# Counts added by VectorE and transposed by a DMA, and the first layer's output added to x in DRAM by a DMA of GpSimd

## The chip, the cores and the metric

The kernel runs on one core of one Trainium2 chip. The metric is the device time of one execution in microseconds (us), lower is better. The engines are TensorE (PE in the rows, its weight loads PEld), VectorE (DVE), ScalarE (ACT), GpSimd (POOL) and SyncE (SP, which here only issues DMAs).

## What is computed

x has 1250 rows (nodes) of 1024 values, and 20,000 edges go from `src` to `dst`, each of one of two relations. Two graph layers follow one another:

```
h = relu(layernorm(x))                       # layer 1, RGCN with 286 hidden columns
g = t5_norm(h)
z = g @ W_root + bias + sum over r of (sum of g[src] @ W_rel[r] over the edges of r into a node) / max(count, 1)
x1 = x + h + elu(z) @ wo_weight              # x + h is called xh below
h2 = relu(layernorm(x1)) @ W                 # layer 2, graph attention
w(s, d) = exp(-leaky_relu(al[s] + ar[d]))    # once for each edge from s to d
out = x1 + elu(sum of w(s, d) * h2[d] / sum of w(s, d))
```

## The kernel before

**Tiles and counts.** The 1250 rows are ten tiles of 125 (`T`, `TILES`). The kernel does not gather edges. For every tile t of destinations TensorE builds a matrix of counts, how often source s points to destination d in relation r, from one-hot rows that VectorE makes (`rows_of`, two comparisons a group, five groups a tile, `one_hots(g)`). The products of a group (`counted(g)` on TensorE, line 1301) land in one of two PSUM banks. ScalarE copies them out as `adj_hi` (line 579, what the sums of messages use) and casts that copy to 16 bits as `adj_16` (line 583). The group after next needs the bank, so it waits for the first of these copies.

**Layer 1.** A pipeline over the ten tiles, written out by hand with a lag for each stage. In one step TensorE does, in this order: group 0 of tile t; `y_transposed` of tile t-2; `summed(0)` of t-1 (messages of relation 0, line 1340); group 1; `summed(1)`; the first part of the transposed counts of t-1; group 2; the first half of `output1` of t-2 (elu(z) @ wo_weight, lines 1385 to 1388); the second part; group 3; the second half of `output1`; the third part; group 4. Sums of a tile need all five copies of its groups. VectorE computes z (`z_of`) when the sums are there, ScalarE takes its exponential (`elu`), VectorE finishes y (`y_of`), TensorE transposes it and both engines copy it out in two precisions (`y_split`).

**Transposed counts.** The attention layer needs the counts of both relations together, and with sources along the free dimension. In the kernel before TensorE transposes them by multiplying with an identity (`counts_transposed`, line 1363, 20 matrix products a tile in parts of 8, 8 and 4, in PSUM banks 4 and 5, both relations adding up in the bank) and ScalarE copies the three parts to `counts` (`counts_out`, line 599).

**x1.** `xh` lies in DRAM (`xh_scratch`). SyncE loads a tile of it into `xt`, VectorE adds the output of layer 1 from PSUM (`output1`, line 1008), SyncE stores the sum in `x1_scratch`. Layer 2 loads it as `x1t`, and again at the end as `xr`.

**Between the layers.** After the pipeline come written-out calls for the last tiles (`before` is tile 8, `last` is tile 9), mixed with the first two tiles of layer 2: norms (`norm2`, line 629), transposes (`transposed2`, line 1397) and the splitting of the eight blocks of W in two precisions, a cast by ScalarE (line 617) and a difference by VectorE (line 1014). The blocks are loaded by SyncE in the order of `ORDER`: two after `rows_free`, four after the last sums, and the last two and `a_b` after the last transposed counts, since they lie where `adj_16` lay. `products2` (lines 1414 to 1416) then takes the blocks one by one. The transposes of layer 2's tile 2 stand behind `products2` of tile 0 on TensorE.

Of the kernel before, what the change touches and what calls it, by code (L numbers as in the profile page):

```python
# [5 lines left out]
def rgcn_gat_kernel(nc, x, src, dst, edge_type, ln_weight, w_rel, w_root, conv_bias, wo_weight, w_gat, a_gat, out):  # L6
# [5 lines left out]
    N, D = x.shape  # L12
# [93 lines left out]
    spans_dram = nc.dram_tensor("spans_scratch", [SPANS, SPAN], F32, kind="Internal").ap()  # L106
    xh_dram = nc.dram_tensor("xh_scratch", [N, D], F32, kind="Internal").ap()
    x1_dram = nc.dram_tensor("x1_scratch", [N, D], F32, kind="Internal").ap()
# [3 lines left out]
    with ctx:  # L112
# [7 lines left out]
        ident_r = sb(ctx, "ident_r", [P, P], R32)  # L120
# [24 lines left out]
        sb(first_rows_of, "below_ring_first", [P, 3 * N], BF16)  # L145
        ring_first = sb(first_rows_of, "ring_first", [P, FIRST, GW, HOT], BF16)
        first_rows_of.close()
        counts = sb(ctx, "counts", [T, TILES, N], U16)
# [16 lines left out]
        def over(name, within, new, shape):  # L165
# [28 lines left out]
        (adj_lo,), lo_end = lay(at, ("adj_lo", [T, BLOCKS, PAIR], R32))  # L194
        (ring_more, adj_16, ident_16), end2 = lay(at, ("ring_more", [P, MORE, GW, HOT], BF16), ("adj_16", [T, BLOCKS, PAIR], F16),
                                                  ("ident_16", [P, P], F16))
# [41 lines left out]
        def columns(adj, b, g):  # L238
# [9 lines left out]
            last_in list_rdy list_out spans_out xlist_in picks_rdy rows_rdy span_rdy win_in wkeyp_rdy found_rdy total_rdy win_16 hot_ready x_ready dot_rdy  # L248
# [3 lines left out]
        for n in ("x_in", "x_ahead", "xh_out", "xh_ahead", "xb_in", "x1_in", "xr_in", "x1_out", "out_done"):  # L252
            S[n] = [sem(f"{n}{b}") for b in range(2)]
# [23 lines left out]
        def _(sp):  # L277
# [58 lines left out]
            def load_xh(t, b):  # L336
                if t < 2:
                    sp.wait_ge(S["xh_out"][b], came_x(TILES - 2 + b, b))
                else:
                    if t < AHEAD:  # L340
                        sp.wait_ge(S["xh_ahead"][b], 32)
                    sp.wait_ge(S["x1_out"][b], came(t - 2, b))
                move(xt[b], row(xh_dram, t), ("xb_in", b))

            def store_x1(t, b):
                sp.wait_ge(S["x1_rdy"], data(t))
                move(row(x1_dram, t), xt[b], ("x1_out", b))

            def load_x1(t, b):
                sp.wait_ge(S["gT_ps"], room(t))  # L350
                sp.wait_ge(S["x1_out"][b], came(t, b))
                move(x1t[b], row(x1_dram, t), ("x1_in", b))
# [3 lines left out]
            load_xh(0, 0)  # L356
            load_xh(1, 1)
# [6 lines left out]
            for t in range(TILES):  # L364
                if t == 4:
                    load_x1(0, 0)
                    load_x1(1, 1)
                if t == TILES - 2:
                    sp.wait_ge(S["rows_free"], 1)
                    for k in ORDER[0:2]:  # L370
                        load_wg(k)
                    load_x1(2, 0)
                    sp.wait_ge(S["s_ps"], data(TILES - 1))
                    for k in ORDER[2:6]:
                        load_wg(k)
                    sp.wait_ge(S["c_ps"], 3 * data(TILES - 1))
                    for k in ORDER[6:8]:
                        load_wg(k)
                    for first, end in ((0, BAND), (BAND, T)):
                        sp.dma_start(a_b[first:end], a_gat.rearrange("o (s d) -> (o s) d", s=2).partition_broadcast(end - first)).then_inc(S["a_in"], 16)  # L380
                if t == TILES - 1:
                    load_x1(3, 1)
                store_x1(t, t % 2)
                if t + 2 < TILES:
                    load_xh(t + 2, t % 2)
# [8 lines left out]
            def load_xr(t, b):  # L394
                sp.wait_ge(S["out_done"][b], out_room(t, b))
                move(xr[b], row(x1_dram, t), ("xr_in", b))
# [18 lines left out]
        def _(pool):  # L415
# [42 lines left out]
            pipeline((residual, 0), steps=(TILES - 2, TILES))  # L458

# [15 lines left out]
        def _(act):  # L475
# [60 lines left out]
            def pads():  # L536
                A.copy(ident_r[:], ident[:])
# [31 lines left out]
            def counts_evicted(t, b, g, usual=False):  # L569
# [5 lines left out]
                if g == 0:  # L575
                    act.wait_ge(S["s_ps"], room(t))
                    act.wait_ge(S["c_ps"], 3 * room(t))
# [17 lines left out]
            def counts_out(t, b, d, parts=range(3)):  # L595
                for c in parts:
                    act.wait_ge(S["c_ps"], 3 * t + c + 1 + 3 * CREDIT)
                    n = min(4, TILES - 4 * c)
                    A.copy(counts[:, bass.ds(t, 1), 4 * T * c:4 * T * c + n * T].rearrange("p o (n s) -> p (o n) s", s=T),
                           ps[0:T, 4 + c % 2, 0:n * CB].rearrange("p (n s) -> p n s", s=CB)[:, :, 0:T]).then_inc(S["c_used"], 1)  # L600

# [10 lines left out]
            act.sem_inc(S["c_used"], 2 * CREDIT)  # L612

# [25 lines left out]
            def counts_part(c):  # L639
                return lambda t, b, d: counts_out(t, b, d, (c,))  # L640

# [3 lines left out]
            def projected(t, b, d):  # L645
                act.wait_ge(S["diag_rdy"], data(t))
                A.copy(h_hi[:, bass.ds(t, 1), :].rearrange("p o (h n) -> p (o h) n", h=2),
# [8 lines left out]
            def early_weights():  # L656
                act.wait_ge(S["first_v"], 1)
# [35 lines left out]

            with act.If_eq(flag, 0):
                act.wait_ge(S["g_ps"], data(TILES - 1))
                A.copy(ident_16[:], ident[:])
# [19 lines left out]
            with act.If_ne(flag, 0):  # L716
                split_wo()
                with act.Fori(0, TILES // 2) as d:
# [3 lines left out]
                    for b in range(2):  # L722
                        for stage in (counts_out, elu, y_split):
                            stage(d * 2 + b, b, d)
# [787 lines left out]
```

## Time and profile before

| | |
|---|---|
| time, median of 3 runs | 532.98 us (532.26 to 533.81) |
| the profiled execution, its own time | 530.4 us |
| span of its instructions | 528.6 us |
| mean granted clock of TensorE | 0.994 |
| TensorE busy | 502.6 us, 95% |
| VectorE busy | 368.9 us, 70% |
| ScalarE busy | 231.3 us, 44% |
| GpSimd busy | 74.6 us, 14% |

The span runs from the first to the last instruction; the time of the execution has 1.8 us more around it. The preparation and the first products fill the span up to about 119 us, the pipeline of layer 1 runs from there to 240 us, its end is mixed with the start of layer 2 up to about 271 us, and from there on TensorE works through layer 2. A row of the timeline gives start, duration, engine, line and operation, and in brackets how long the engine was idle before it and who ended that.

### The profile page before, as it was taken

The numbers are of one execution on the slowest core, as the hardware profiler recorded it, in microseconds if no ns is written. First come the engines' busy times: TensorE is split into PE (matmuls) and PEld (weight loads), VectorE is DVE, ScalarE is ACT, GpSimd is POOL, SyncE is SP. The second block draws the span as 40 slices with busy tenths as digits, with TensorE's granted clock in tenths as the row PEclk, the third lists the DMA queues.
The fourth block names the chain that finished last, engine by engine and source line by source line (L and its number), as shares of the span: only waits on it lengthen the run. The fifth ranks groups of instructions, "written<-read, shape, count | busy, mean of one in ns | idle before, by whom it ended". The sixth has DMA issues, their size and how long they took to land.

```text
span 528.6 us, 7977 instructions
## 1 busy us (share of the span) xinstructions
PE 502.6 (95%) x3073; PEld 433.2 (82%) x3073; DVE 368.9 (70%) x634; ACT 231.3 (44%) x386; POOL 74.6 (14%) x72
## 2 busy tenths in 40 slices
PE   3989999997899999998999999999999999999995
PEld 2889989997789999998778888888787888888885
DVE  4836885578798888855875555554798887777633
ACT  5855443407856666668733332221333322222112
POOL 1362213100000000000000000000073322222400
PEclk9999999999899999999999999999999999999998
DMA  9862273304013233225951111100022222222211
GB/s 259 223 224 79 78 236 104 118 1 110 1 50 107 81 120 115 79 79 167 311 191 39 40 39 40 39 1 0 1 78 79 78 78 79 78 79 78 79 41 41
DMA packets 22186, 49.15 MB, mean 93 GB/s; under 512 B 4798, under 2 KB 10709, under 8 KB 22018
## 3 DMA queue, kind: packets, MB, share of 16 engines
q1 hardware_dynamic: 21887, 48.33, 30.5%
q8 instruction: 26, 0.43, 0.3%
q0 software_dynamic: 256, 0.26, 0.2%
q14 instruction: 17, 0.14, 0.1%
HBM read 33.05 MB, written 16.85 MB: 94 GB/s over the span
## 4 chain that ended last, share of the span: by engine, by line
PE 84%; DVE 8%; ACT 5%; issue 1%; DMA 1%; SPq 0%; DVEq 0%; ACTq 0%
PE ps L1208 13%; PE ps L1433 9%; PE ps L1340 9%; PE ps L1434 9%; PE ps L1435 9%; PE ps L1414 6%; PE ps L1416 6%; PE ps L1415 6%; PE ps L1301 3%; PE ps L1363 2%; PE ps L1385 2%; PE ps L1397 1%; PE ps L1387 1%; PE ps L1386 1%; PE ps L1234 1%
## 5 line engine op out<-in xcount | busy, mean ns | idle before, releaser
L1433 PE MATMUL ps<-h_hi,att_hi 125*125 125x512 f32 (+1 forms) x190 | 73.5, 387 | 0.0
L1434 PE MATMUL ps<-h_lo,att_hi 125*125 125x512 f32 (+1 forms) x190 | 72.6, 382 | 0.0
L1435 PE MATMUL ps<-h_hi,att_lo 125*125 125x512 f32 (+1 forms) x190 | 72.5, 382 | 0.0
L1414 PE MATMUL ps<-wg,gT_hi 128*125 128x512 f32 x160 | 64.0, 400 | 0.5 <-DVE wg L1014 0.4
L1416 PE MATMUL ps<-wg,gT_lo 128*125 128x512 f32 x160 | 63.1, 394 | 0.0
L1415 PE MATMUL ps<-wg,gT_hi 128*125 128x512 f32 x160 | 63.0, 394 | 0.0
L1340 PE MATMUL ps<-msg_hi,adj_hi 125*125 125x288 f32 x200 | 56.9, 308 | 0.6 <-ACT adj_hi L579 0.5
L1340 PE MATMUL ps<-msg_lo,adj_hi 125*125 125x286 f32 x200 | 51.7, 297 | 0.0
L1208 PE MATMUL ps<-w_hi,hT_hi 128*125 128x430 f32 x128 | 46.5, 363 | 0.1
L1208 PE MATMUL ps<-w_hi,hT_lo 128*125 128x430 f32 x128 | 45.9, 358 | 0.0
L1208 PE MATMUL ps<-w_lo,hT_hi 128*125 128x430 f32 x128 | 45.7, 357 | 0.0
L465 POOL TENSOR_TENSOR some<-first_att 125x625 f32<-125x625 f32 x1 | 2.4, 2445 | 289.9 <-DVE first_att L1072 289.9
L1435 PEld LDWEIGHTS ps<-h_hi,att_lo 125*125 125x125 f32 x190 | 35.3, 186 | 7.9
L1434 PEld LDWEIGHTS ps<-h_lo,att_hi 125*125 125x125 f32 x190 | 35.2, 185 | 7.5
L1433 PEld LDWEIGHTS ps<-h_hi,att_hi 125*125 125x125 f32 x190 | 35.2, 185 | 7.4
L1340 PEld LDWEIGHTS ps<-msg_hi,adj_hi 125*125 125x125 f32 x200 | 37.8, 189 | 1.7 <-ACT adj_hi L579 1.2
L676 ACT ACTIVATE em<-ps,rinv 125x512 f32<-125x512 f32 (+1 forms) x21 | 14.0, 668 | 56.4 <-DVE hp L1124 56.4
L1340 PEld LDWEIGHTS ps<-msg_lo,adj_hi 125*125 125x125 f32 x200 | 36.9, 190 | 0.0
L1414 PEld LDWEIGHTS ps<-wg,gT_hi 128*125 128x125 f32 x160 | 29.7, 185 | 8.8 <-DVE wg L1014 1.8
L1048 DVE CUSTOM_DVE_ANT_0 h_lo<-ps,a_b 125x1024 fp32r<-125x1024 f32 x20 | 24.5, 1224 | 16.8 <-PE ps L1416 16.4
L1416 PEld LDWEIGHTS ps<-wg,gT_lo 128*125 128x125 f32 x160 | 29.7, 185 | 7.3
L1415 PEld LDWEIGHTS ps<-wg,gT_hi 128*125 128x125 f32 x160 | 29.7, 186 | 6.9
(203 smaller groups left out, 1058.8 us busy)
## 6 DMA issues: line engine op xcount, KB each, us to landing
xt<-in_x SPq DMA_DIRECT2D x10, 448.0 KB
xh_scratch<-xt SPq DMA_DIRECT2D x10, 448.0 KB
xt<-xh_scratch SPq DMA_DIRECT2D x10, 448.0 KB
x_scratch<-xt SPq DMA_DIRECT2D x10, 448.0 KB
x1t<-x_scratch SPq DMA_DIRECT2D x10, 448.0 KB
xr<-x_scratch SPq DMA_DIRECT2D x10, 448.0 KB
out_x<-xr SPq DMA_DIRECT2D x19, 224.0 KB
wg_raw<-in_L_gnn_W SPq DMA_DIRECT2D x8, 512.0 KB, 9.1
```

What stands on the lines that cost most here:

```text
L676: A.activation(em[b][:, first:end], heads(b, h, (first, end)), ACT.Exp, scale=rinv[b][:, 0:1]).then_inc(S["el_rdy"], 1)
L1048: V.tensor_tensor_reduce(out=halves(h_lo[:, TILES - 1, :]), in0=hps, in1=halves(a_b[:, s, :]), scale=1.0, scalar=0.0, op0=ALU.mult, op1=AL ...
L1208: last = M.matmul(out, lhsT, rhs, start=(n == 0), stop=(n == len(terms) - 1))
L1301: last = M.matmul(win_bank(n, x), srcs, wide, start=c == 0, stop=c == SLOTS - 1)
L1340: last = M.matmul(*product, start=(s == 0 and n == 0), stop=(end and n == 1), skip_group_check=True)
L1363: last = M.matmul(to[s], part[:, r * TILES + s, mine], unit, start=(s == some[0] and r == 0), stop=(r == RELS - 1), skip_group_check=True)
L1414: M.matmul(to, hi, wg[k][:, 0, cut], start=n == 0, stop=False)
L1415: M.matmul(to, hi, wg[k][:, 1, cut], start=False, stop=False)
L1416: last = M.matmul(to, lo, wg[k][:, 0, cut], start=False, stop=n == KT - 1)
L1433: M.matmul(to, hi[:, s, :], h_hi[:, s, cut], start=s == 0, stop=False)
L1434: M.matmul(to, hi[:, s, :], h_lo[:, s, cut], start=False, stop=False)
L1435: return M.matmul(to, lo[:, s, :], h_hi[:, s, cut], start=False, stop=s == TILES - 1)
```

## The change

**Counts.** VectorE adds the two relations of a tile in 16 bits (`summed` of the vector block, 125 x 1250 values into `sum_16`, which has 128 x 10 x 128 places and is set to zero before the first). It stands in front of `z_of` and waits for the casts of the tile and for the landing of the DMA of the tile before. ScalarE issues one DMA with transpose for a tile (`counts_turned`), from `sum_16` to `counts`, one step later, between the copies of group 2 and `elu`. The three parts of `counts_transposed` on TensorE and of `counts_out` on ScalarE are gone from the usual path, and `adj_16` now holds unsigned integers.

**x1.** ScalarE copies the output of layer 1 from PSUM to `xt` (`output1`, at the end of a step). GpSimd issues two DMAs for a tile that add `xt` to `xh_scratch` in DRAM (`output_added`), waits until they have landed and raises `x1_done`, which ScalarE waits for before it uses the same buffer two tiles later. SyncE's loads of `xt`, VectorE's addition and SyncE's stores go away; layer 2 reads `xh_scratch`.

**Order.** The loads of the last two blocks of W and of `a_b` wait for the landing of all ten transposes (`ct_out`). The transpose of the last tile is issued by ScalarE behind its copy of the last output and ahead of the casts of six blocks of W. `ident_r` is set up only on the path that is not taken here.

```diff
+            def output_added(t, b, d):
+                pool.wait_ge(S["x1_rdy"], data(t))
+                for first, end in ((0, BAND), (BAND, T)):
+                    G.dma_start(row(xh_dram, t)[first:end], xt[b][first:end], accum_op=ALU.add).then_inc(S["x1_out"][b], 16)
+                pool.wait_ge(S["x1_out"][b], came(t, b))
+                pool.sem_inc(S["x1_done"], 1)
...
+            def counts_turned(t, b, d):
+                act.wait_ge(S["sum_16"], data(t))
+                act.dma_start(counts[:, t], sum_16[:].rearrange("p n s -> p (n s)"), transpose=True).then_inc(S["ct_out"], 16)
...
+            def output1(t, b, d):
+                act.wait_ge(S["o_ps"], data(t))
+                act.wait_ge(S["x1_done"], room(t))
+                A.copy(xt[b][:].rearrange("p (h n) -> p h n", h=2), ps[0:T, 6:8, :]).then_inc(S["x1_rdy"], 1)
...
-                pipeline((counted(0), 0), (y_split, 2), (counted(1), 0), (counts_part(0), 1), (counted(2), 0), (elu, 1), (counts_part(1), 1),
-                         (counted(3), 0), (counts_part(2), 1), (counted(4), 0), opening=split_wo, before=2, steps=(0, TILES))
+                pipeline((counted(0), 0), (y_split, 2), (counted(1), 0), (counted(2), 0), (counts_turned, 1), (elu, 1),
+                         (counted(3), 0), (counted(4), 0), (output1, 2), opening=split_wo, before=2, steps=(0, TILES))
                 act.sem_inc(S["rows_free"], 1)
...
                 norm2(0, 0)
-                counts_part(0)(*last)
                 norm2(1, 1)
                 transposed2(0, 0, 0)
                 back_to_exp()
-                counts_part(1)(*last)
                 elu(*last)
-                counts_part(2)(*last)
+                output1(*before)
                 y_split(*last)
                 split_gat_weights(range(0, 2))
                 transposed2(1, 1, 0)
+                output1(*last)
+                counts_turned(*last)
                 second_layer()
...
+            def summed(t, b, d):
+                mine = slice(T * b, T * (b + 1))
+                dve.wait_ge(S["win_16"], done(nth(t, NG - 1)))
+                if t == 0:
+                    V.memset(sum_16[:], 0).then_inc(S["pad_rdy"], 1)
+                    dve.wait_ge(S["pad_rdy"], 1)
+                else:
+                    dve.wait_ge(S["ct_out"], 16 * t)
+                V.tensor_tensor(sum_16[0:T, :, 0:T], adj_16[:, 0:TILES, mine], adj_16[:, TILES:BLOCKS, mine], ALU.add).then_inc(S["sum_16"], 1)
...
-                pipeline((one_hots(0), 0), (one_hots(1), 0), (y_split, 3), (one_hots(2), 0), (z_of, 2), (one_hots(3), 0), (y_of, 2),
-                         (one_hots(4), 0), (lambda t, b, d: split_wo() if t == 0 else None, 2), (output1, 3), steps=(0, TILES))
+                pipeline((one_hots(0), 0), (one_hots(1), 0), (y_split, 3), (one_hots(2), 0), (summed, 2), (z_of, 2), (one_hots(3), 0), (y_of, 2),
+                         (one_hots(4), 0), (lambda t, b, d: split_wo() if t == 0 else None, 2), steps=(0, TILES))
...
-                pipeline((counted(0), 0), (y_transposed, 2), (summed(0), 1), (counted(1), 0), (summed(1), 1), (counts_part(0), 1), (counted(2), 0),
-                         (output1(0), 2), (counts_part(1), 1), (counted(3), 0), (output1(1), 2), (counts_part(2), 1), (counted(4), 0), steps=(0, TILES))
+                turned = lambda t, b, d: y_transposed(t, b, d, True)
+                pipeline((counted(0), 0), (turned, 2), (summed(0), 1), (counted(1), 0), (summed(1), 1), (counted(2), 0),
+                         (output1(0), 2), (counted(3), 0), (output1(1), 2), (counted(4), 0), steps=(0, TILES))
```

## Rows read from the trace of the kernel before

**Rows 1.** The page: busy time of the engines, and shares of the chain that ended last.

```profile
PE 502.6 (95%) x3073; PEld 433.2 (82%) x3073; DVE 368.9 (70%) x634; ACT 231.3 (44%) x386; POOL 74.6 (14%) x72
...
PE 84%; DVE 8%; ACT 5%; issue 1%; DMA 1%; SPq 0%; DVEq 0%; ACTq 0%
```

**Rows 2.** Busy time by stretch, one step: length; PE, PEld, DVE, ACT, POOL; clock; DMA.

```profile
190.60:203.30 12.70, 12.70 (x129) 11.79 (x129) 10.80 (x22) 8.17 (x18) 0.00 (x0) 1.00 0.56 163
```

**Rows 3.** Timeline of TensorE in that step: start, us, what.

```profile
196.38 0.62 PE L1363 MATMUL ps<-ident,adj 125*125 125x126 f16 x8
...
196.84 0.62 PE L1301 MATMUL ps<-ring 128*128 128x100 bf16 x10
...
201.60 0.39 PE L1363 MATMUL ps<-ident,adj 125*125 125x126 f16 x4
...
201.83 1.07 PE L1301 MATMUL ps<-ring 128*128 128x100 bf16 x20
```

**Rows 4.** Timeline of ScalarE in that step.

```profile
197.51 0.59 ACT L579 CAST adj_hi<-ps 125x500 fp32r<-125x500 f32 x1
...
198.14 0.64 ACT L583 CAST adj<-adj_hi 125x500 f16<-125x500 f32 x1
...
198.68 0.44 ACT L604 ACTIVATE eb<-eb 125x286 f32<-125x286 f32 x1
...
202.49 0.59 ACT L579 CAST adj_hi<-ps 125x500 fp32r<-125x500 f32 x1
```

**Rows 5.** Timeline of VectorE in that step.

```profile
196.58 0.16 DVE L977 TENSOR_SCALAR deg<-ps 125x2 f32<-125x2 f32 x1 [1.30 <-PE ps L1340]
...
201.80 1.23 DVE L1008 TENSOR_TENSOR xt<-ps,xt 125x1024 f32<-125x1024 f32 x1 [0.26 <-PE ps L1388]
```

**Rows 6.** Groups by line over the span: busy us, mean ns, idle before.

```profile
L898 DVE TENSOR_TENSOR ring<-wkey,iota 128x1280 bf16<-128x1280 f16 x32 | 26.1, 817 | 0.0
...
L1104 DVE TENSOR_TENSOR att_lo<-att,att_hi 125x1250 fp32r<-125x1250 f32 x9 | 13.4, 1488 | 10.4 <-ACT att_hi L669 10.4
...
L599 ACT CAST counts<-ps 125x500 uint16<-125x500 f32 x20 | 11.4, 572 | 20.7 <-PE ps L1363 20.7
...
L647 ACT CAST h_hi<-ps 125x1024 fp32r<-125x1024 f32 x10 | 10.2, 1015 | 56.4 <-DVE diag L1052 56.4
```

**Rows 7.** SyncE's tile moves by source line: issue ns min/median/max, and landing.

```profile
L280 SPq DMA_DIRECT2D x_scratch<-xt x20: 303/370/408, 153.8 to 260.9; - x20
...
DMA to landing us min/median/max: 3.7/4.4/5.3
```

**Rows 8.** DMA issues: count, KB each, median us from issue to landing.

```profile
spans_scratch<-list_scratch SPq DMA_DIRECT2D x1, 1296.0 KB, 7.7
...
win<-spans_scratch,span_of POOLq DMA_INDIRECT x2, 4.1
```

**Rows 9.** Timeline of SyncE: issue of the move in 1296 rows of 1 KB.

```profile
70.62 1.07 SPq L325 DMA_DIRECT2D spans_scratch<-list_scratch x1
```

**Rows 10.** Timeline, start of the pipeline of layer 1.

```profile
131.17 0.16 DVE L977 TENSOR_SCALAR deg<-ps 125x2 f32<-125x2 f32 x1 [0.94 <-PE ps L1340]
...
152.37 0.40 PE L1340 MATMUL ps<-msg_hi,adj_hi 125*125 125x288 f32 x1
```

**Rows 11.** Timeline, from layer 1 to layer 2.

```profile
244.38 1.24 ACT L629 ACTIVATE x1t<-x1t,stats 125x1024 f32<-125x1024 f32 x1 [0.24 <-DVE stats L1032]
...
258.40 0.39 PE L1388 MATMUL ps<-wo_mix,yT_hi 96*125 96x512 f32 x1
...
265.37 1.05 ACT L617 CAST wg<-wg_raw 128x1024 fp32r<-128x1024 f32 x1 [1.29 <-DMA wg_raw<-in_L_gnn_W]
266.43 1.28 ACT L625 ACT_TABLE_LOAD   x1
...
268.33 1.22 DVE L1014 TENSOR_TENSOR wg<-wg_raw,wg 128x1024 fp32r<-128x1024 f32 x1
...
271.10 1.02 PE L1397 MATMUL ps<-ident,x1t 125*128 125x125 f32 x8
```

More of the change, by code:

```diff
@@ L363, in _ @@
                 sp.dma_start(wo_rest[j * FR:(j + 1) * FR, :], wo_weight[2 * FT:F, :]).then_inc(S["wo_in"][2], 16)
[L364 to L385, printed above, removed]
+            load_x1(0, 0)
+            load_x1(1, 1)
+            sp.wait_ge(S["rows_free"], 1)
+            for k in ORDER[0:2]:
+                load_wg(k)
+            load_x1(2, 0)
+            sp.wait_ge(S["s_ps"], data(TILES - 1))
+            for k in ORDER[2:6]:
+                load_wg(k)
+            sp.wait_ge(S["ct_out"], 16 * TILES)
+            for k in ORDER[6:8]:
+                load_wg(k)
+            for first, end in ((0, BAND), (BAND, T)):
+                sp.dma_start(a_b[first:end], a_gat.rearrange("o (s d) -> (o s) d", s=2).partition_broadcast(end - first)).then_inc(S["a_in"], 16)
+            load_x1(3, 1)
             for t in range(4, TILES):
@@ L395, in load_xr @@
                 sp.wait_ge(S["out_done"][b], out_room(t, b))
[L396 removed]
+                move(xr[b], row(xh_dram, t), ("xr_in", b))
             def store(t, b):
@@ L722, in _ @@
                     for b in range(2):
-                        for stage in (counts_out, elu, y_split):
+                        for stage in (counts_out, elu, y_split, output1):
                             stage(d * 2 + b, b, d)
+                act.sem_inc(S["ct_out"], 16 * TILES)
                 act.sem_inc(S["rows_free"], 1)
@@ L1167, in _ @@
                 z_of(*last)
+                summed(*last)
                 y_of(*last)
-                output1(*before)
                 y_split(*last)
@@ L1343, in summed, with counts_transposed @@
                 return relation
-            def counts_transposed(more, parts=range(3)):
-                def tile(t, b, d):
+            def counts_transposed(t, b, d):
                     mine = slice(T * b, T * (b + 1))
-                    for c in parts:
+                    for c in range(3):
                         if c == 0:
-                            pe.wait_ge(S["win_out" if more else "win_16"], done(nth(t, NG - 1)))
+                            pe.wait_ge(S["win_out"], done(nth(t, NG - 1)))
                         if c != 1:
```

100 lines of the change are left out of this document (46 added, 54 removed).

## The prediction

> **What bounds the kernel now.** I read the page first: TensorE is busy for 95% of the span, and 84% of the chain that ended last runs through it [rows 1]. Then the windows, one step of layer 1's pipeline at a time: steps repeat every 12.70 us, and TensorE is busy for all of it, while VectorE works 10.80 and ScalarE 8.17 us [rows 2]. So in the steady steps only TensorE's own work counts. The timelines of the three engines show how near the others are: VectorE sits idle for 1.30 us before z, for TensorE's sums [rows 5]. At both ends of the pipeline this is different. At its start VectorE's z waits for TensorE but is itself waited for [rows 10], and at its end TensorE is fed by ScalarE's norms and by the splitting of W, whose last cast waits 1.29 us for its DMA [rows 11]. After that TensorE runs without gaps to the end, so a delay of its transposes at 271.10 [rows 11] moves the end by as much.
>
> **The counts: what goes.** On TensorE the parts with 8 products take 196.84 - 196.38 = 0.46 us of the stream each, the part with 4 takes 201.83 - 201.60 = 0.23 [rows 3]: 1.15 us a tile, 11.5 us for ten. On ScalarE the copies go, two of 0.57 and a shorter one [rows 6], 1.5 us a tile.
>
> **What VectorE gains and loses.** Its addition to x (1.23, [rows 5]) goes. The sum of two 16-bit operands of 1250 values is in no row. From below, the 16-bit comparison of 1280 values takes 0.82; from above, the 32-bit subtraction of 1250 values takes 1.49 [rows 6]. I take 0.8, since operand width is what the two differ in. It falls in the 1.30 us before z [rows 5], so even 1.49 delays z by only 0.2. VectorE's load becomes 10.80 - 1.23 + 0.8 = 10.4 (at most 11.1) of a step of 12.70 - 1.15 = 11.55: it stays under TensorE. Queued behind its new wait for the landing are z, two comparisons and y; the transpose has most of a step to land before that bites.
>
> **What ScalarE gains.** The copy of two PSUM banks to `xt` is like that of `h_hi`, 1.02 us [rows 6]. Its busy time becomes 8.17 - 1.5 + 1.0 = 7.7, plus the issue of the transpose, which holds the engine's queue. Where it stands matters more than the load. From the start of group 2's copy to that of group 4's are 202.49 - 197.51 = 4.98 us; TensorE gets from group 2 to group 4 sooner by 0.46 + 0.23, so 4.29 stay. Between them lie two pairs of copies of 1.15 each and the exponential of 0.44 [rows 4], 2.74 in all. An issue of up to 1.5 us is hidden; up to 2.1 if it can run under the cast of 0.64 ahead of it. Each microsecond more delays group 4's copy, which the sums of the tile wait for, and costs its length in seven steps.
>
> **The price of the issue.** No row has a transpose. The shortest plain issue takes 0.30 us [rows 7]. The nearest in pieces is the move in 1296 rows, 1.07 us [rows 9]; the transpose reads 128 partitions times 10 blocks, 1280 pieces of 256 B. From above I take ten blocks, each as dear as an issue of its own between the shortest and the median of these rows, 0.30 to 0.37: 3.3 us. I take 1.1. For the landing, tile moves take 3.7 to 5.3, median 4.4 [rows 7], and the 1296 rows took 7.7 [rows 8], though from DRAM to DRAM. I take 4.4. In a steady step the landing is hidden either way.
>
> Rows bound this price and don't show it. The Trainium skill, "DMA: Bandwidth & Descriptors", lists in the section Why a DMA increments its semaphore by 16 and not by 1 that a transpose from SBUF to SBUF of 8,192 tiles took 262,144 cycles of the issuing sequencer before its newest generation, 32 a tile. With tiles of 16 rows by 128 columns this case has 80 of them, an estimated 2.1 us at ScalarE's 1.2 GHz, and the saving below would fall to some 1.7 us; with the 256-byte tiles that the section SDMA does more than copy names it has 1280, over 30 us a step. Its section Latency and other measured facts puts a transpose's rate at 261 GB/s, by which 328 KB would need only 1.3 us. No row here decides between them.
>
> **x1 through DRAM.** SyncE loses its loads and stores of `xt`. GpSimd is idle in these stages [rows 2]; an indirect DMA of its own landed in 4.1 us [rows 8]. Two issues and a landing stand against the two steps (23 us) until ScalarE uses the buffer again, so I cost it at nothing in the steps. Even 15 us would be hidden there. At the end tile 9's sum is first needed deep in layer 2.
>
> **The start.** ScalarE and VectorE set the pace until the sums at 152.37 [rows 10]. In front of the first z now stand the zeroing and the first addition, some 2.2 us where 0.94 was idle, and in front of the next z another 0.8 without a gap to hide in. ScalarE can pass neither, since the transpose waits for the sum. It gains its copies of counts. Worked through the order of the queues, the sums of 152.37 start 0.35 later. From there seven steps save 1.15 each: 8.05 - 0.35 = 7.7 us at the end of the pipeline.
>
> **The way into layer 2.** Here the change gives time back. First, ScalarE copies tile 7's output, 1.02 us, before it gets to the norm at 244.38 [rows 11], for which TensorE already waits, and tile 8's before the last `y_split`. The removed parts of counts only lengthen TensorE's wait. The last product of layer 1 (258.40, ending 258.79) comes 0.9 later, on the clock of before. Second, the last transpose. Counted from the end of these products: ScalarE issues after 0.1; landing 4.4; SyncE issues the last two blocks of W, 0.4; they land after 4.4 + 1.1 for the second; cast 1.05; table load 1.28; square root 0.3; reciprocals 0.4; VectorE's difference 1.22; TensorE's six products 1.5. In all 16.15 us to the transposes of tile 2. Before, these were 271.10 - 258.79 = 12.3 [rows 11]. That gives 3.9, with the 0.9 a loss of 4.8.
>
> **Sum.** 7.7 - 4.8 = 2.9 us. The profiled execution of 530.4 becomes 527.5. The median of the runs is 2.6 above that execution, so 532.98 - 2.9 = 530.1 us. With landings of 3.7 it is 529.4, with 7.7 about 533.4. With an issue of 0.3, 529.8; with 2.1, 531.3.
>
> **Rivals.**
>
> *The transpose holds ScalarE (slower).* At 3.3 us of issue the excess over 2.1 is 1.2 in seven steps, 8.4; with a start later by 0.9 and a last landing later by 2.2 the result is 530.1 + 11.5 = about 542. It decides from 2.5 us on. For it: the transpose stands in the one part of the step with little room [rows 4]. Against it: the plain issue in as many pieces, 1.07 [rows 9]. Chance 0.27. The far end of it: each 16 partitions of each block an issue of their own, 80 at 0.30 [rows 7] or 24 us, less 2.1 hidden, in nine steps: some 197 us more, about 730. Chance 0.03, since the 1296 rows did not cost that. That is the side on which the Trainium skill's count of cycles a tile lies, as cited above, and the trace has nothing on it.
>
> *The way into layer 2 eats the rest (no difference).* The two blocks of W land behind 1 MB of `a_b` traffic or the transpose lands in 7.7: the loss there is 7 to 8 instead of 4.8, time about 533. For it: ScalarE already waited for these loads [rows 11]. Chance 0.16.
>
> *The blocks come early enough (faster).* Six of the eight no longer share the DMA engines with stores of x1; if the last two land together in about 2 us after issue and the first norm isn't late, the loss is 2: 527.4. Against it: no landing in rows 7 is under 3.7. Chance 0.10.
>
> *The change does nothing.* If VectorE had been the bound, TensorE's saved time would become idle time; its 1.30 us of waiting [rows 5] speaks against it. Chance 0.04.
>
> **Chances and range.** My forecast has 0.40. A measurement here tells 0.3%, 1.6 us, from no change. Faster by more: the forecast but for landings above 5 (0.38) and the early blocks (0.10), with a little of the third rival: 0.49. Within: 0.20. Slower: 0.31. The range takes in the early blocks below (526) and the rival with 3.3 us above (542). The likeliest case alone has 529 to 532.
>
> **What would show it.** Steady steps of 11.55 us with TensorE busy throughout confirm the first part; ScalarE's transposing issue of 1.1 us and no wait of TensorE for line `adj_hi` the second. Longer steps with TensorE waiting for that copy mean the first rival. Between the last product of layer 1 and the transposes of tile 2 should lie 16 us with two waits of ScalarE for W. I would be wrong if VectorE waited for `ct_out` in the steps: then the transfer itself takes 9 us or more, which no row excludes.

## The result, and the profile after

The changed kernel takes 534.94 us (median of 20 runs, 532.13 to 541.72), the kernel before 532.06 us in the same sessions (20 runs, 529.28 to 534.72). The ratio is 1.005, with a 95% interval of 1.0033 to 1.0067: slower, by 0.3 to 0.7%. I had forecast a gain of 2.9 us and got a loss of 2.9. The profiled execution took 534.8 us with a span of 533.0; before it was 530.4 and 528.6.

The page after, busy time by engine (to [rows 1]):

```profile
PE 496.6 (93%) x2873; PEld 423.2 (79%) x2873; DVE 369.3 (69%) x635; ACT 226.8 (43%) x364; POOL 91.5 (17%) x92
```

TensorE does 200 instructions and 6.0 us of busy time less than in [rows 1], and yet the span is 4.4 us longer. So more than 10 us of it is new idle time, and the windows say where. Columns as in [rows 2]; the last but two is the granted clock:

```profile
125.00:130.00 5.00, 4.75 (x31) 4.67 (x32) 3.47 (x6) 1.95 (x4) 0.00 (x0) 0.66 0.04 12
135.00:140.00 5.00, 2.14 (x18) 1.90 (x19) 2.99 (x6) 4.46 (x7) 0.00 (x0) 0.87 0.34 66
140.00:145.00 5.00, 5.00 (x38) 4.92 (x38) 4.47 (x5) 4.94 (x10) 0.00 (x0) 0.79 0.00 0
175.00:230.00 55.00, 55.00 (x516) 49.41 (x515) 45.09 (x95) 36.51 (x71) 8.27 (x10) 1.00 0.48 82
235.00:240.00 5.00, 2.90 (x20) 2.67 (x20) 1.32 (x7) 4.73 (x9) 1.66 (x2) 1.00 0.76 241
240.00:245.00 5.00, 4.67 (x25) 4.68 (x26) 1.26 (x2) 3.94 (x6) 0.00 (x0) 0.66 0.69 175
265.00:270.00 5.00, 2.01 (x7) 1.03 (x6) 1.76 (x4) 3.56 (x5) 0.00 (x0) 0.84 0.96 247
270.00:275.00 5.00, 4.03 (x13) 3.33 (x14) 1.99 (x2) 1.06 (x1) 0.00 (x0) 0.50 0.06 16
```

The steady part, 175 to 230 us, is as forecast: TensorE busy for 55 of 55 us at full clock. The trouble is at both ends. Between 235 and 245 and again between 265 and 275 us TensorE first waits, and then works at a clock of 0.66 and 0.50 of full; 0.50 is the lower of its two levels, 1.2 instead of 2.4 GHz, for the whole stretch. The kernel before had these rows at the same times, with one low stretch of its own at the start:

```profile
135.00:140.00 5.00, 3.89 (x24) 3.72 (x25) 2.81 (x5) 4.94 (x10) 0.00 (x0) 0.66 0.00 0
...
240.00:245.00 5.00, 4.06 (x43) 3.81 (x41) 2.50 (x9) 4.45 (x10) 0.00 (x0) 1.00 0.33 102
...
270.00:275.00 5.00, 5.00 (x28) 4.10 (x27) 2.83 (x6) 0.84 (x1) 0.00 (x0) 1.00 0.44 143
```

ScalarE's timeline after, a steady step and then the way into layer 2 (to [rows 4] and [rows 11]):

```profile
195.19 0.59 ACT L570 CAST adj_hi<-ps 125x500 fp32r<-125x500 f32 x1 [1.94 <-PE ps L1315]
195.81 1.36 ACTq L595 DMA_TRANSPOSE counts<-sum  x1
...
206.80 0.59 ACT L570 CAST adj_hi<-ps 125x500 fp32r<-125x500 f32 x1 [1.93 <-PE ps L1315]
...
235.51 1.00 ACT L612 COPY xt<-ps 125x1024 f32<-125x1024 f32 x1
...
239.03 2.37 ACT L634 ACTIVATE x1t<-x1t,stats 125x1024 f32<-125x1024 f32 x2 [0.24 <-DVE stats L1047]
...
254.81 1.37 ACTq L595 DMA_TRANSPOSE counts<-sum  x1
...
264.70 1.05 ACT L622 CAST wg<-wg_raw 128x1024 fp32r<-128x1024 f32 x1 [4.59 <-DMA wg_raw<-in_L_gnn_W]
266.74 1.05 ACT L622 CAST wg<-wg_raw 128x1024 fp32r<-128x1024 f32 x1 [0.99 <-DMA wg_raw<-in_L_gnn_W]
```

Between the two copies of group 2 lie 206.80 - 195.19 = 11.61 us, one step. The transpose holds the queue for 1.36 us, and in the steps nobody waits for it. At the end of layer 1 the copy of tile 7's output (L612) stands ahead of the norms, and the last transpose ahead of two long waits for W. The chain that ended last joins the two, start, us, what:

```profile
254.81 3.40 DMA counts<-sum
...
258.60 8.12 DMA wg_raw<-in_L_gnn_W
```

TensorE's side, its longest wait at the start and then the way into layer 2:

```profile
137.74 0.63 PE L1315 MATMUL ps<-ring 128*128 128x100 bf16 x10 [3.18 <-ACT adj_hi L570]
...
240.32 1.25 PE L1411 MATMUL ps<-ident,x1t 125*128 125x125 f32 x8 [2.42 <-ACT x1t L634]
...
267.06 0.49 PE L1425 MATMUL ps<-wg,gT_hi 128*125 128x512 f32 x1 [1.87 <-DVE wg L1029]
...
270.97 0.79 PE L1425 MATMUL ps<-wg,gT_hi 128*125 128x512 f32 x1 [2.10 <-DVE wg L1029]
...
273.69 1.77 PE L1411 MATMUL ps<-ident,x1t 125*128 125x125 f32 x8
```

The last row answers to 271.10 of [rows 11]. The same eight transposes took 1.02 us there and take 1.77 us here, after the wait.

A figure beside the trace: in the 20 timed runs of the changed kernel the mean granted clock of the span is 0.982 (0.973 to 0.986); in four sets of 17, 31, 29 and 26 runs of the kernel before it is 0.990 to 0.991. Within the runs of each kernel time and clock go together (correlation -0.88 after, -0.81 to -0.92 before).

### The profile page after: what moved, and what is told of

Its sections match the earlier page's. It is cut to its first block, busy times and chain, and to the rows that moved or that the text cites. A ratio compares the mean times of both kernels' runs of the same rounds, so it can differ in the third digit from the quotient of the medians.

```text
span 533.0 us, 7561 instructions
## 1 busy us (share of the span) xinstructions
PE 496.6 (93%) x2873; PEld 423.2 (79%) x2873; DVE 369.3 (69%) x635; ACT 226.8 (43%) x364; POOL 91.5 (17%) x92
## 4 chain that ended last, share of the span: by engine, by line
PE 81%; DVE 7%; ACT 6%; DMA 3%; issue 2%; ACTq 0%; SPq 0%; DVEq 0%
PE ps L1222 12%; PE ps L1354 9%; PE ps L1444 9%; PE ps L1446 9%; PE ps L1445 9%; PE ps L1425 6%; PE ps L1427 6%; PE ps L1426 6%; PE ps L1315 3%; PE ps L1399 2%; PE ps L1411 2%; PE ps L1401 2%; PE ps L1400 2%; DMA wg_raw<-in_L_gnn_W 2%; PE ps L1248 1%
## 5 line engine op out<-in xcount | busy, mean ns | idle before, releaser
L1354 PE MATMUL ps<-msg_hi,adj_hi 125*125 125x288 f32 x200 | 59.8, 320 | 0.9 <-ACT adj_hi L570 0.8
L1354 PE MATMUL ps<-msg_lo,adj_hi 125*125 125x286 f32 x200 | 54.2, 308 | 0.0
L440 POOL DMA_DIRECT2D xh_scratch<-xt x20 | 16.8, 980 | 145.8 <-ACT xt L612 140.8
L1354 PEld LDWEIGHTS ps<-msg_hi,adj_hi 125*125 125x125 f32 x200 | 40.0, 200 | 2.1 <-ACT adj_hi L570 1.6
L1425 PEld LDWEIGHTS ps<-wg,gT_hi 128*125 128x125 f32 x160 | 30.0, 187 | 14.3 <-DVE wg L1029 7.4
L570 ACT CAST adj_hi<-ps 125x500 fp32r<-125x500 f32 x50 | 29.2, 584 | 28.0 <-PE ps L1315 27.3
L1354 PEld LDWEIGHTS ps<-msg_lo,adj_hi 125*125 125x125 f32 x200 | 39.1, 201 | 0.0
```

Of the source, the lines that this page charges most:

```text
L440: G.dma_start(row(xh_dram, t)[first:end], xt[b][first:end], accum_op=ALU.add).then_inc(S["x1_out"][b], 16)
L570: A.copy(columns(adj_hi, b, g), bank_of).then_inc(S["win_out"], 1)
L1354: last = M.matmul(*product, start=(s == 0 and n == 0), stop=(end and n == 1), skip_group_check=True)
L1425: M.matmul(to, hi, wg[k][:, 0, cut], start=n == 0, stop=False)
```

## The experiments

The theory that I took from the traces: the loop gains what I said, and both ends give it back, in waits of TensorE and in the lower clock behind them; the largest piece is the last transpose, behind which the last two W blocks are issued. Rivals: the transposes themselves cost; x1's new way costs; the W blocks land late by contention whatever their issue; the clock's fall has nothing to do with it.

No experiment runs the transposing DMA itself: in the kernels called "plain" a plain DMA of the same bytes stands in its place, so that layer 2 reads counts that are not transposed. All comparisons are with the kernel before.

### 1. The x1 part alone

From the kernel before; counts stay on TensorE.

```
-  (DVE)  V.tensor_tensor(xt[b], ps[0:T, 6:8, :], xt[b], ALU.add)
+  (ACT)  A.copy(xt[b], ps[0:T, 6:8, :])          # last in a step, lag 2
+  (POOL) G.dma_start(row(xh_dram, t), xt[b], accum_op=ALU.add)
```

> The x1 part of the change alone: counts are transposed by TensorE in three parts as before; the output is copied by ScalarE two steps later and added to xh in DRAM by GpSimd's DMA. Theory: the steps stay at 12.7 us, bound by TensorE, the loop gives nothing, and the way into layer 2 loses about 1 us by the copy ahead of the normalisations, with some of it again by a lower granted clock after the wait: 533 to 535 us, ratio 1.002 to 1.006. Rival (freeing SyncE and VectorE of x1 is worth something by itself, since the last W blocks are issued earlier): 530 us or less. Rival (the accumulating DMAs cost by contention): 537 us or more, with longer landings of W.

Measured: 533.79 us (12 runs), ratio 1.0023, interval 1.0007 to 1.0039. TensorE's wait for the norm, 0.38 us in the kernel before, is 1.31:

```profile
249.68 1.07 PE L1392 MATMUL ps<-ident,x1t 125*128 125x125 f32 x8 [1.31 <-ACT x1t L628]
```

That is the 0.9 us which ScalarE's output copy costs ahead of the norms. The two rivals are out: no gain from the freed queue, and no 537. So x1 alone costs 0.2%, at no gain in the steps; with the counts moved as well it costs more (experiment 5), so that the parts don't simply add up.

### 2. A plain DMA for the transpose

```
-  act.dma_start(counts[:, t], sum_16[:], transpose=True)
+  act.dma_start(counts[:, t], sum_16[:])
```

> The changed kernel with ScalarE's transposing DMA replaced by a plain DMA of the same 128x1280 elements from and to the same tiles, so that the counts which layer 2 reads are not transposed; all else is left. Theory (the transpose is hidden in the steps, and the loss is in TensorE's waits at both ends of the loop): the steps stay at 11.6 us, the start and the output copy ahead of layer 2's normalisations lose what they lost (sums of the fourth tile's step about 1.4 us later than before, the wait before layer 2's first transposes about 2.4 us); a shorter issue and landing bring the last two W blocks 1 to 3 us earlier: 531.5 to 534 us, ratio to before 0.999 to 1.004. Rival (the transposes themselves cost, by holding ScalarE's queue or the DMA engines): 529 us or less. Rival (a plain DMA costs the same at issue and landing, and nothing hangs on them): 534.5 to 535.5 us.

Measured: 531.58 us (12 runs), ratio 1.0011, interval 0.999 to 1.0033, inside the theory's range. The issue takes 0.47 instead of 1.37 us and the last landing 2.47 instead of 3.40:

```profile
138.04 0.63 PE L1315 MATMUL ps<-ring 128*128 128x100 bf16 x10 [2.26 <-ACT adj_hi L570]
```

```profile
255.13 2.47 DMA counts<-sum
...
257.99 8.00 DMA wg_raw<-in_L_gnn_W
266.01 1.05 ACT wg L622
```

The last W block still lands at 266.0, 0.7 us earlier than with the transpose, and the span is 532.5 instead of 533.0. These times hide something: TensorE's first group of counts starts at 118.33 us in the profile of the changed kernel and at 119.84 in this one, and nothing ahead of it differs between the two kernels. Counted from there, the last W block lands 2.2 us earlier without the transpose and the span ends 2.0 us earlier, which is the 0.4% by which the ratios differ (their intervals just touch). Two places show it. The last landing is 0.9 us shorter. And at the start of the loop the first transpose holds ScalarE's queue for 1.53 us, ScalarE is idle for 0.94 us before it loads the table for its exponential, and TensorE's wait before the third tile's first group of counts is 3.18 us, where it is 2.25 to 2.26 in this profile and in those of experiments 3 and 5 to 8. So the transposes do cost something by themselves, some 2 us by these two profiles. The mean clock of the runs differs too, 0.988 here and 0.982 there, and what part of the 0.4% is the clock stays open.

### 3. The last one early

```
                 y_split(*last)
+                counts_turned(*last)
                 split_gat_weights(range(0, 2))
                 transposed2(1, 1, 0)
                 output1(*last)
-                counts_turned(*last)
```

> As the plain kernel (counts moved and not transposed), and ScalarE issues the last of these DMAs right behind the last split of y, no longer behind the output copy of tile 9, some 4 us earlier. Theory (the late W blocks, and the clock after those waits): the last two W blocks are issued 3 to 4 us earlier, the waits before the last two blocks of products (1.87 and 2.10 us in the changed kernel) fall to under 1 us, the granted clock of the stretch behind them stays near 1, layer 2's third tile is transposed 2 to 4 us earlier than in the plain kernel, and the time falls by as much: ratio to before 0.993 to 0.998. Rival (the blocks come late by contention with the other W blocks, which are in flight till 264 us, not by issue): less than 1 us.

Measured: 527.79 us (12 runs), ratio 0.9932, interval 0.9908 to 0.9957. One line of ScalarE's order is worth 0.8%, some 4 us, and makes of a kernel that is no faster than the one before a faster one. The chain:

```profile
246.72 5.71 DMA counts<-sum
252.82 6.71 DMA wg_raw<-in_L_gnn_W
```

And TensorE, with its windows:

```profile
239.24 0.97 PE L1411 MATMUL ps<-ident,x1t 125*128 125x125 f32 x7 [2.43 <-ACT x1t L634]
...
263.79 0.50 PE L1425 MATMUL ps<-wg,gT_hi 128*125 128x512 f32 x1 [0.27 <-DVE wg L1029]
...
265.28 1.02 PE L1411 MATMUL ps<-ident,x1t 125*128 125x125 f32 x8
```

```profile
240.00:245.00 5.00, 5.00 (x33) 4.58 (x32) 3.13 (x8) 3.03 (x6) 0.00 (x0) 1.00 0.71 180
...
265.00:270.00 5.00, 5.00 (x27) 4.10 (x27) 3.45 (x7) 1.02 (x1) 0.00 (x0) 1.00 0.47 134
```

The waits before the last two blocks of products are down to 0.27 us, the clock behind them is 1.00, the transposes are back at 1.02 us. One thing speaks against a simple rule: the wait of 2.43 us before the first transposes is the same as in the plain kernel, where the clock from 240 to 245 us was 0.69, and here it is 1.00. A wait of this length can bring the clock down and need not.

### 4. TensorE kept busy in its waits

```
+  def fill(n, times):
+      for _ in range(times):
+          M.matmul(bank(n, T, 512), wo_hi[:, 0, 0:T], wo_hi[:, 0, 0:512], start=True, stop=True)
   summed(0)(*last)
+  fill(4, 10)
   transposed2(0, 0, 0)
   ...                                   # products2(0), before block n
+  fill(2, {2: 4, 4: 2, 6: 8, 7: 9}.get(n, 0))
   pe.wait_ge(S["wg_rdy"], n + 1)
```

> As the plain kernel, with 33 idle products of 127x512 on TensorE, 0.23 us each at full clock, 7.7 us in all, whose output nobody reads: 10 before layer 2's first transposes, and 4, 2, 8 and 9 before the third, fifth, seventh and eighth block of products of layer 2's first tile, where the changed kernel's TensorE waits. Theory (work after these waits runs at half clock because TensorE waited): the granted clock stays at 1 from 235 to 280 us and the kernel is 1 to 3 us faster than the plain one, though it does 7.7 us more work. Rival (the clock's fall there has nothing to do with the waits): equal to the plain kernel or slower by up to 5 us, with the clock low again.

The same three stretches, first of the plain kernel:

```profile
240.00:245.00 5.00, 4.38 (x24) 4.39 (x25) 1.26 (x2) 4.24 (x6) 0.00 (x0) 0.69 0.82 187
...
265.00:270.00 5.00, 1.41 (x7) 0.79 (x5) 1.27 (x3) 3.54 (x4) 0.00 (x0) 0.92 1.00 272
270.00:275.00 5.00, 4.76 (x15) 4.02 (x16) 1.95 (x4) 0.32 (x1) 0.00 (x0) 0.50 0.10 29
```

and of the filled one:

```profile
240.00:245.00 5.00, 4.90 (x35) 4.32 (x34) 1.86 (x5) 4.20 (x6) 0.00 (x0) 1.00 0.77 183
...
265.00:270.00 5.00, 3.82 (x17) 2.70 (x15) 1.11 (x3) 3.38 (x4) 0.00 (x0) 1.00 0.93 227
270.00:275.00 5.00, 4.59 (x24) 3.85 (x25) 3.18 (x7) 0.54 (x2) 0.00 (x0) 1.00 0.24 66
```

In the profiled execution the clock stays at full, and the transposes of tile 3 start at 284.08 instead of 286.60, 2.5 us earlier with 33 products more. Over the runs this gain is not there: 532.24 us (12 runs), ratio 1.0008, interval 0.9985 to 1.0032, the same as the plain kernel's 1.0011. The forecast of 1 to 3 us faster missed. What stands is weaker: 7.7 us of added work cost nothing that 12 runs can show. The profile alone doesn't tie the clock to the waits, since experiment 3 has the same wait of 2.43 us and a full clock behind it without any filling. The means over the runs point that way: 0.990 with the products and 0.988 without, a difference of 0.002 with an interval of about the same size. Experiments 11 and 12 show it better.

### 5. The counts part alone, with the plain DMA

x1 as in the kernel before, the last DMA right behind the copy for the transposes of tile 1.

```
-  output1(*last)          # ACT copy, and its POOL DMA
   transposed2(1, 1, 0)
   counts_turned(*last)
```

> The counts part of the change alone with the plain DMA in place of the transposing one (counts not transposed); x1 is added by VectorE and loaded and stored by SyncE as in the kernel before. Theory (the output copy on ScalarE ahead of the normalisations, and at the start, is part of the loss): the steps stay 11.6 to 11.8 us, the wait before layer 2's first transposes shrinks by about 1 us against the plain kernel, the last DMA is issued some 2 us earlier; 1.5 to 4 us faster than the plain kernel: ratio to before 0.992 to 0.998. Rival (the counts part holds the loss): no faster than the plain kernel. Rival (VectorE becomes the bound of a step with its output add and the new sum): steps over 12 us and 535 us or more.

Measured: 527.52 us (8 runs), ratio 0.9917, interval 0.989 to 0.9945. TensorE's wait for the norm shrinks from 2.43 to 1.51 us, the last DMA is issued at 249.23 instead of 255.13:

```profile
249.23 6.45 DMA counts<-sum
256.06 4.91 DMA wg_raw<-in_L_gnn_W
```

Against the plain kernel's 1.0011 that is 0.9%, just beyond the expected range. It is the x1 part that pushed the last DMA back, by the copy of tile 9's output in front of it.

### 6. The norms first

On the kernel of experiment 3.

```
-  (output1, 2)                                    # tile 7's copy in the last step
+  (lambda t, b, d: output1(t, b, d) if t < TILES - 3 else None, 2)
   norm2(1, 1)
+  output1(TILES - 3, 1, 3)
   transposed2(0, 0, 0)
```

> The plain kernel with the early last DMA, and ScalarE's output copy of tile 7 behind layer 2's first two normalisations, no longer ahead of them. Theory (the copy ahead of the norms is what lengthened TensorE's wait before layer 2's first transposes): that wait shrinks from 2.43 by about 1.0 us, layer 1's last product comes 1 us earlier, ratio to before 0.991 to 0.993 where the kernel without it has 0.9932. Rival (the norms are set by the normalisations' statistics or the table load): the wait stays at 2.4 us and the ratio at 0.993. Rival (the copy is now late for TensorE's output of tile 8): a new wait of up to 1 us there, ratio 0.993 to 0.995.

Measured: 529.51 us (12 runs), ratio 0.9965, interval 0.994 to 0.999. The theory is right about the place and wrong about the time. TensorE's wait for the norm falls to 1.51 us, and another appears:

```profile
238.09 1.07 PE L1412 MATMUL ps<-ident,x1t 125*128 125x125 f32 x8 [1.51 <-ACT x1t L634]
...
266.06 0.50 PE L1426 MATMUL ps<-wg,gT_hi 128*125 128x512 f32 x1 [3.17 <-DVE wg L1030]
```

```profile
245.94 7.94 DMA counts<-sum
254.27 7.53 DMA wg_raw<-in_L_gnn_W
```

The last DMA of counts is issued 0.8 us earlier than in experiment 3 and lands 1.5 us later: 7.94 instead of 5.71 us in flight. GpSimd's add of tile 7 now starts at 240.36 and that of tile 8 at 248.06, where they were at 235.72 and 247.57, so the first of them has moved close to the loads of W, whose last six are issued from 241.8 on. I had listed contention as a rival of the late issue; here both seem to act. That it is GpSimd's adds that collide is not shown: in experiment 5, which has none, the last DMA took 6.45 us.

### 7. The start

On the kernel of experiment 3.

```
-  dve.sem_inc(S["sum_16"], CREDIT)       # behind VectorE's first stage
+  "sum_16" among the credits given at VectorE's start
-  (DVE)  V.memset(sum_16[:], 0)          # in the first step
+  (POOL) G.memset(sum_16[:], 0)          # ahead of the loop
```

> The plain kernel with the early last DMA; the semaphore credit of the sum is given at VectorE's start instead of behind its work of the first stage, and the zeroing of the sum's tile is done by GpSimd ahead of the loop, no longer by VectorE in the first step. Theory (these two are what the start lost): the 1.26 us wait of TensorE before the second group of counts goes back to the 0.61 us of the kernel before, VectorE's first z comes 0.6 us earlier, the sums of the fourth tile come 0.8 to 1.4 us earlier: ratio to before 0.990 to 0.992. Rival (the start's loss is ScalarE's copies and the clock after the waits, which other runs show with every order): no change, 0.993.

Measured: 525.89 us (6 runs), ratio 0.9907, interval 0.9874 to 0.994. The point estimate is as forecast; the interval overlaps that of experiment 3, so the gain is seen in the trace rather than in the ratio: counted from the first group of counts, the group of counts that TensorE starts at 151.00 us comes 0.5 us earlier than in experiment 3 (0.8 to 1.4 were forecast), and its wait before the second group of counts goes from 1.26 to 0.70 us.

```profile
119.92 0.63 PE L1315 MATMUL ps<-ring 128*128 128x100 bf16 x10 [0.70 <-ACT adj_hi L573]
```

ScalarE's first cast of counts had waited for a credit which VectorE gave late; no step of my prediction had that wait.

### 8. Both together

> The last two edits together on the plain kernel with the early last DMA. Theory: their gains add, 1.0 us from the normalisations and 0.8 to 1.4 us from the start, 526 us, ratio to before 0.989 to 0.991. Rival (either is only argued): the ratio of the better one of the two.

Measured: 529.28 us (12 runs), ratio 0.9947, interval 0.992 to 0.9975. It missed. As in experiment 6 the last DMA of counts takes long to land, 8.08 us, and TensorE waits 2.08 us before the last block. But the profiled execution took 526.48 us, as forecast, so its trace can't show what the median lost. The 12 runs go from 524.53 to 530.69 us, with clocks from 0.996 down to 0.983.

### 9. The sum on VectorE, the transposition left on TensorE

If a loop step is worth 1.1 us, half of it can be had without a transposing DMA. From the kernel before, output as in the reference:

```
+  V.tensor_tensor(sum_16[:], adj_16[:, 0:TILES, mine], adj_16[:, TILES:BLOCKS, mine], ALU.add)
-  for r in range(RELS): M.matmul(to[s], adj_16[:, r * TILES + s, mine], ident_16, ...)
+  M.matmul(to[s], sum_16[:, s, :], ident_16, ...)
```

> The kernel before with VectorE's sum of the two relations' counts (in float16), and the transposition left on TensorE, 10 instead of 20 products for each tile; x1 as before; the first third of the last tile's counts moved behind the first relation's sums. The output is the reference's. Theory (a step is bound by TensorE and VectorE has room): TensorE's counts parts fall from 1.15 to about 0.6 us for a tile, the steps from 12.70 to 12.15 us, the loop gives 5 us, and the ways in and out of it are those of the kernel before but for the sum's 0.8 us at the start: 527 to 529 us, ratio 0.990 to 0.994. Rival (VectorE's add is late for TensorE in a step, or VectorE, at 70% busy, becomes the bound): steps of 12.4 us or more and a ratio of 0.996 to 1.002.

Measured: 531.98 us (12 runs), ratio 1.0005, interval 0.9982 to 1.0027. The steps are 12.13 us, as in the theory; the time is the rival's, and what takes it is not a step but the start:

```profile
147.93 0.44 PE L1378 MATMUL ps<-ident,sum 125*125 125x126 f16 x4 [3.90 <-DVE sum L970]
```

```profile
138.63 2.36 DVE L978 TENSOR_TENSOR wo_lo<-wo_raw,wo_hi 127x1024 fp32r<-127x1024 f32 x2 [2.06 <-ACT wo_hi L594]
...
147.06 0.81 DVE L970 TENSOR_TENSOR sum<-adj 125x1250 f16<-125x1250 f16 x1
```

Tile 1's sum stood behind VectorE's split of the output weights. Its inputs had been there since 137.6 us. (The profiled execution, 528.0 us, is the fastest of the twelve.)

### 10. That sum moved ahead

```
-  (lambda t, b, d: split_wo() if t == 0 else None, 2)
+  (lambda t, b, d: (summed(1, 1, 0), split_wo()) if t == 0 else None, 2)
```

> The kernel with the sum on VectorE and the transposition on TensorE, and the sum of the second tile put in front of VectorE's split of the output weights, which held it back by 9 us so that TensorE waited 3.90 us for it at 147.9 us. Theory (that wait, and the clock of 0.93 and 0.73 in the ten us around it, are the whole of what that kernel lost of its 5 us): no wait there, clock 1 from 145 to 155 us, 3 to 5 us faster than the former one, ratio to before 0.991 to 0.995. Rival (another limit of the start takes the place, ScalarE's copies or VectorE's split): 0.998 to 1.000.

Measured: 529.29 us (10 runs), ratio 0.9946, interval 0.9921 to 0.9971, the ratio that the theory gave, though the step from experiment 9 is 2.7 us and not 3 to 5. The wait of 3.90 us is gone, and this kernel, which computes what the reference does, beats both.

### 11 and 12. Filling the start

```
+  for _ in range(17):      # at the head of the third step
+      M.matmul(bank(6, T, FP), adj_hi[:, 0, 0:T], msg_hi[:, 0, 0, :], start=True, stop=True)
```

> The kernel before with 17 idle products of 125x288 on TensorE, 0.13 us each at full clock, 2.3 us in all, put ahead of the first group of counts of the third tile, where TensorE waits 2.42 us for ScalarE at the start of the loop; their output is overwritten and the kernel's output is the reference's. Theory (after such a wait TensorE's granted clock falls to 0.5 or 0.66 for about 5 us, and the work behind it pays): the clock from 135 to 140 us stays at 1 in the profiled run, and the kernel gets 0.5 to 1.7 us faster though it does 2.3 us more work: ratio 0.997 to 0.999. Rival (the fall has nothing to do with the wait, or the mean over runs is set elsewhere): 1.000, and the clock falls in that stretch as before.

> The last kernel with the 17 idle products in TensorE's 2.7 us wait ahead of the third tile's first group of counts. Theory (clock after the wait): 0.5 to 1.7 us faster than without them, ratio to before 0.989 to 0.993. Rival: equal to it.

Measured: on the kernel before 532.25 us (12 runs), ratio 0.9991, interval 0.9968 to 1.0015, no difference. On experiment 10's kernel 528.38 us (11 runs), ratio 0.9933, interval 0.9903 to 0.9963, the fastest kernel here with the reference's output, but not told apart from 0.9946. In the profile of the first the clock behind the filled wait is 1.00, and it had fallen already before it:

```profile
125.00:130.00 5.00, 4.88 (x24) 4.66 (x22) 4.46 (x7) 2.28 (x5) 0.00 (x0) 0.50 0.16 36
...
135.00:140.00 5.00, 4.80 (x60) 4.32 (x58) 3.98 (x8) 4.91 (x10) 0.00 (x0) 1.00 0.00 0
```

TensorE had waited 0.5 to 0.6 us four times before 125 us, as in the kernel before, whose profile has 1.00 in this stretch. Where the clock falls at the start varies from one execution to the next, so the profile doesn't decide.

The runs do, for the mean granted clock. It rises from 0.991 to 0.994 with the products, by 0.0029 with a 95% interval of 0.0014 to either side (26 and 12 runs), and from 0.991 to 0.994 on experiment 10's kernel, by 0.0031 and 0.0019 (10 runs each, fast ones). The 2.3 us of products at full clock can lift a mean over 530 us by 0.00004 at most, so it is the work around them that got more clock: TensorE's idle time in this gap lowers the clock on average. 0.003 of the span is 1.6 us; both medians moved the right way by 0.1%, which is within the noise.

## Why the prediction was wrong, step by step

**The counts: what goes** was right. 1.10 us a step (12.70 to 11.60) against 1.15, TensorE busy throughout. Experiment 2 has the same steps.

**What VectorE gains and loses** was right: the sum takes 0.81 us, I took 0.8; VectorE never waits for `ct_out`.

**The price of the issue** was right enough in the steps: 1.37 us (1.27 to 1.60) against 1.1, at the median under the 1.5 that lie hidden; it landed in 3.4 us (3.3 to 5.9) against 4.4. The rival with 3.3 us is out. At the start the issue was not hidden (experiment 2). The Trainium skill's count, "DMA: Bandwidth & Descriptors", section Why a DMA increments its semaphore by 16 and not by 1, which I had read as 80 tiles of 32 cycles, an estimated 2.1 us, is 0.7 above the measured 1.37 and of its order; the reading by 256-byte tiles, over 30 us, is not borne out.

**x1 through DRAM** at nothing in the steps was right; GpSimd's adds landed in 4.9 us. At nothing altogether it was wrong. Alone it costs 0.2% (experiment 1), and without it the kernel with the plain DMA is 0.9% faster (experiment 5): its copies on ScalarE stand ahead of the norms and of the last transpose. Whether its DMAs also delay those of W is not shown.

**The start** failed: the sums of the fourth tile's step start at 153.78, 1.4 us later than at 152.37 [rows 10], where I had 0.35. Counted from the first group of counts (118.33 and 118.76) it is 1.8. I missed the late credit, 0.6 us (experiment 7), and the first transpose's hold on ScalarE's queue, 0.9 us of TensorE's time (experiment 2). The clock here is not shown to be a cost of the change: it was 0.66 from 125 to 130 us where the profile before had 1.00, but the kernel of experiment 11, which up to there is the kernel before, has 0.50, and the profile before has its 0.66 ten us later. At the end of the loop 6.3 us were left of 7.7.

**The way into layer 2** is the step that failed. I had 0.9 us for the copy ahead of the norms. Layer 1's last product ended 4.03 us earlier than before instead of 6.3, a loss of 2.3: the wait for the norm became 2.42 us, and the sums behind it took 4.00 us instead of 2.88 at a clock of 0.66. From there to the transposes of tile 2 I had 16.15 us; it took 18.9. The last transpose was issued when I said and landed in 3.4 us as against 4.4, but the last W block landed 8.1 us after its issue, where I had 4.4 and 1.1 for being second, and from that landing to the transposes it took 7.0 us instead of 5.75, with TensorE's products at half clock. The term for W is the one mis-sized most, by 2.6 us, and it was avoidable: I took it from x's tile moves [rows 7], while the trace before has a row for W's own eight loads:

```profile
L355 SPq DMA_DIRECT2D wg_raw<-in_L_gnn_W x8: 328/432/701, 245.1 to 253.8; - x8
...
DMA to landing us min/median/max: 6.3/9.1/11.5
```

What held the last block in flight is not isolated; the 1000 KB of `a_b`, which one of my rivals names, were issued 1.1 us behind it. The order on ScalarE's queue I had priced, and did not ask what another was worth: the sum of tile 9 was ready at 248.1 and was issued at 254.8, and that is 0.8% (experiment 3). In all the way took 2.27 + 6.62 = 8.9 us where I had 4.8. Behind the transposes of tile 2 another 1.8 us went, which I had put at nothing; 1.3 of it is TensorE's wait for the first `att_lo` of layer 2, 2.1 us where it was 0.8. 6.3 - 8.9 - 1.8 is the span's -4.4.

**The missing term** is the clock. My sum ran every instruction at the speed of the profile before. The mean clock of the runs went from 0.990 to 0.982. As time of the span that is 0.010 * 532 = 5.3 against 0.018 * 535 = 9.6 us not granted, 4.3 more; an upper bound for its share in the miss of 5.8, since part of the low stretches is idle anyway. That TensorE's idle time lowers it on average is shown by the runs with filled waits, by 0.002 to 0.003 (experiments 4, 11 and 12); that every wait does it is refuted (experiment 3), and the size of its part in the median stays open. Of the rivals, the one in which the way into layer 2 eats the rest, with a loss of 7 to 8 us there, was nearest; of its two reasons the late landing of W came true and the transpose's landing in 7.7 did not.

## What to carry to other kernels

A gain in the steady steps of a pipeline is paid out only at its end: read the order of every queue there, and ask for each instruction when its input was ready and when it is issued. Where a moved step ends in a semaphore that loads are waiting for, look at its last instance first: in the steps nobody waited for the transposes, and the place of the last one alone was worth 0.8%. Take the landing of a load from the rows of that load, in its own crowd, not from a transfer of like size elsewhere.

Add to the sum a term for the clock when the change makes TensorE wait, and take it from several runs: the granted clock of one profile can be 1.00 or 0.50 in the same stretch of the same code. Before two profiles are compared by their times, find where the same instruction starts in both ahead of the change; here that differed by up to 1.8 us.

## What the runs showed of the hardware

A DMA transpose of 128x1280 16-bit elements from SBUF to SBUF holds ScalarE's queue for 1.27 to 1.60 us and lands 3.3 to 5.9 us after its issue; a plain DMA of the same bytes holds it for 0.47 us and lands in 2.7 us in the middle, but in 6.45 us where W's blocks of 512 KB are in flight (experiment 5) and in 8.1 us where GpSimd's adds are too (experiment 8). The adding DMA of GpSimd takes 0.94 us to issue and lands in 4.9 us. Idle products in TensorE's waits, 7.7 us of them, cost no time that the runs can show (1.0008 against 1.0011), and 2.3 us of them at the start raise the mean granted clock of the runs by 0.003.
